# A fused convolution-attention and transformer block: the attention of six images in one run of slots, in place of pairs of images

## The reference

```
# channel attention (8 heads of 24 channels): Gram matrix over the tokens, softmax, projection, residual
q, k, v = split(w_qkv @ x + b_qkv);  attn = softmax(l2norm(q) @ l2norm(k).T * temperature)
x = x + (w_proj @ (attn @ v) + b_proj)
t = tokens(x)                                        # 1024 x 192
# causal self-attention: 6 heads of 32
h = layernorm(t);  q, k, v = h @ Wq, h @ Wk, h @ Wv
att = softmax(where(causal, q @ k.T / sqrt(192), -inf));  t = t + att @ v
# feed-forward with sign weights, two clips by a maximum over a group of 6 images
t = t + quant(gelu(quant(layernorm(t) @ Wb1 + b1)) @ Wb2 + b2)
```

## Time and profile before

| | before |
|---|---|
| time, median of 3 runs | 4978.42 us (4969.53 to 4983.48) |
| the profiled execution: its own time | 4979.79 us |
| its span | 4978.0 us |
| busy PE, DVE, ACT, POOL | 4124.8, 3470.0, 2934.6, 773.7 us |
| mean granted TensorE clock | 0.945 of full |

### The profile page before, as it was taken

One profiled execution on the slowest core, in us unless ns is written; L12 is line 12 of the kernel. 1 busy time (PEld: TensorE's weight loads), 2 busy tenths in 40 slices (PEclk: granted clock), 3 DMA queues, 4 the chain that ended last, 5 costly groups with the idle time before them and its releaser, 6 DMA issues.

```text
span 4978.0 us, 116213 instructions
## 1 busy us (share of the span) xinstructions
PE 4124.8 (83%) x38848; PEld 2997.8 (60%) x38848; DVE 3470.0 (70%) x6999; ACT 2934.6 (59%) x6271; POOL 773.7 (16%) x671
## 2 busy tenths in 40 slices
PE   4988887869898876989887779889876989897778
PEld 2766664556666545766664556666545766664555
DVE  3767677757676786767678767677776767778666
ACT  1555556846555575555566845555575555566745
POOL 0000002600000144000002600000143000002600
PEclk8999998989999998999998989999988999998989
DMA  2111111011121101111111011121101111111011
GB/s 59 40 34 33 34 39 26 0 46 33 34 57 35 33 0 39 33 34 33 40 33 26 0 46 33 37 56 33 33 0 39 33 34 34 39 33 26 0 39 39
DMA packets 46377, 161.59 MB, mean 32 GB/s; under 512 B 10098, under 2 KB 10612, under 8 KB 45684
## 3 DMA queue, kind: packets, MB, share of 16 engines
q1 hardware_dynamic: 45812, 154.38, 13.2%
HBM read 28.52 MB, written 25.17 MB: 11 GB/s over the span
## 4 chain that ended last, share of the span: by engine, by line
issue 78%; POOL 13%; PE 5%; DVE 2%; POOLq 1%; ACT 1%; DMA 0%; SPq 0%; DVEq 0%; ACTq 0%
POOL work L508 7%; POOL hi_z L478 2%; POOL hi_z L497 1%; POOL rstd L473 1%; POOL rstd L493 1%; PE S L691 1%; POOL NK L468 1%; PE PT L763 1%; PE PT L655 1%; PE OUT L675 1%; PE S L699 0%; DVE work L364 0%; DVE nmax L1114 0%; DMA B<-in_b 0%; PE S L641 0%
## 5 line engine op out<-in xcount | busy, mean ns | idle before, releaser
L870 ACT ACTIVATE work<-S,nmax 128x256 f32<-128x256 f32 (+7 forms) x1536 | 1138.8, 742 | 1114.6 <-DVE nmax L1114 1054.8
L1114 DVE TENSOR_REDUCE nmax<-S 128x1 f32<-128x256 f32 (+7 forms) x1536 | 1156.2, 753 | 851.0 <-PE S L643 835.2
L655 PE MATMUL PT<-ident,work 128*128 128x128 f32 x6912 | 1114.5, 282 | 214.8 <-DVE work L364 185.8
L655 PEld LDWEIGHTS PT<-ident,work 128*128 128x128 f32 x6912 | 749.7, 142 | 430.4 <-DVE work L364 260.9
L364 DVE COPY work<-PT 128x512 f32<-128x512 f32 (+3 forms) x1536 | 891.9, 581 | 57.7 <-PE PT L655 52.7
L691 PE MATMUL S<-odd,W1b 128*128 (+1 forms) x2160 | 529.0, 401 | 74.5 <-DVE work L1187 67.0
L508 POOL TENSOR_TENSOR work<-work 128x512 f16<-128x512 f32 x360 | 414.0, 1158 | 147.4 <-ACT work L916 133.0
L691 PEld LDWEIGHTS S<-odd,W1b 128*128 128x128 f16 x2160 | 214.4, 102 | 359.3 <-DVE work L1187 97.7
L641 PE MATMUL S<-KS,QS 128*128 128x512 f16 (+3 forms) x1152 | 334.5, 346 | 104.5 <-issue 56.0
L468 POOL TENSOR_TENSOR NK<-NK,halfneg 96x4 f32<-96x4 f32 x32 | 32.5, 1016 | 2188.0 <-DVE NK L1036 2188.0
L874 ACT ACTIVATE work<-PT 128x512 f32<-128x512 f32 (+3 forms) x768 | 331.3, 431 | 53.5 <-PE PT L655 53.4
(11 more groups left out here) (189 smaller groups left out, 6375.2 us busy)
## 6 DMA issues: line engine op xcount, KB each, us to landing
X<-in_x SPq DMA_DIRECT2D x32, 768.0 KB, 5.4
odd<-hi_z SPq DMA_DIRECT2D x128, 192.0 KB, 4.2
odd<-odd SPq DMA_DIRECT2D x128, 192.0 KB, 4.2
out_y<-work SPq DMA_DIRECT2D x64, 384.0 KB, 3.1
QS<-hi_z SPq DMA_DIRECT2D x64, 192.0 KB, 3.7
QS<-odd SPq DMA_DIRECT2D x64, 192.0 KB, 4.1
KS<-hi_z SPq DMA_DIRECT2D x64, 192.0 KB, 4.7
KS<-odd SPq DMA_DIRECT2D x64, 192.0 KB, 4.7
```

The source lines that it names most:

```text
L655: last = tr(bank[:, P * (j - c0):P * (j - c0) + P], PS[m % 2][:, m // 2 % 2, P * j:P * j + P], ident[:, :])
L870: A(PS[n % 2][:, n // 2 % 2, 0:w], S[:, n % 2, 0:w], ACT.Exp, bias=nmax[:, n % MAXES:n % MAXES + 1], accum_out=rowsum[:, sum_col(n):sum_co ...
L1114: v.tensor_reduce(nmax[:, n % MAXES:n % MAXES + 1], S[:, n % 2, 0:P * (qtile(n) + 1)], AX.X, ALU.max, negate=True).then_inc(max_made, 1)
```

## The change

- The loop body is a group of six images (216 slots for units, then 4 to drain); the last two images have a shorter one. An image has 36 slots.
- A slot holds one large unit or two small ones. Of six slots, four are large units (positions 0, 1, 3, 4), two are pairs of small ones (2, 5): each round of six slots takes the eight units `combos(11 - r)` and `combos(r)`. Each slot has two banks of `S`; the two halves of `S` alternate. One maximum instruction serves both units of a pair.
- TensorE transposes the tiles of slot n-2 at slot n. ScalarE copies the first four tiles of a large unit, ahead of its exponential of the slot; VectorE copies the others and those of the small pairs.
- PV takes four units at a time in four column groups: the four large ones of a round at slot 7 after its start, the four small ones at slot 8. Outputs leave in three batches of 128 x 512 an image, where there were four of 96 x 512.
- The front has the one bank `FR`. Each step waits for the release of the step before it. A step stands at the start of a slot (a whole number in the table: right behind the scores) or at its end (a half). VectorE's part of a `qk` step comes half a slot after TensorE's.
- The first scores of an image wait for both halves of the stacking (`stacked[0]` and `stacked[1]`).
- Tokens of images 1 to 5 of a group are written to T1 directly; QKL moves into XT; the spare part of `odd` holds the small pairs' exponentials.

The core of the diff:

```diff
-TILES = [(1, 7), (3, 5), (0, 6), (2, 4)]
-AHEAD = 3
-PV_AT = (8, 11)
-OT_AT, BACK_AT = 18, 19
+IMAGE = 36
+AHEAD = 2
+LARGES = (0, 1, 3, 4)
+SMALLS = (2, 5)
+PV_AT, OT_AT, BACK_AT = (7, 8), 15, 16
...
+def combos(grp):
+    return [divmod(4 * grp + i, NH) for i in range(4)]
+def slot_units(n):
+    r, p = n % IMAGE // 6, n % 6
+    if p in SMALLS:
+        i = 2 * SMALLS.index(p)
+        return [(r, i), (r, i + 1)]
+    return [(11 - r, LARGES.index(p))]
...
-SLOTS = {"xt0": 0, "xt1": 1, "xt2": 2, "xt3": 4, "g0a": 5, "g0": 6, "g1a": 7, "g1": 8, "wg0": 9, "wg1": 10,
-         "na": 11, "rb": 15, "u": 18, "mt": 19, "t0": 20, "t1": 21, "t2": 22, "t3": 23, "z0": 31, "z1": 32,
-         "z2": 33, "z3": 34, "qk0": 35, "qk1": 36, "qk2": 37, "qk3": 38, "qk4": 39, "qk5": 40, "v0": 41, "v1": 42,
-         "v2": 43, "v3": 44}
+SLOTS = {"xt0": 0, "xt1": 0.5, "xt2": 1.5, "xt3": 2, "g0a": 3, "g0": 3.5, "g1a": 4.5, "g1": 5, "wg0": 6, "wg1": 7,
+         "na": 8, "rb": 10.5, "u": 13.5, "mt": 14.5, "t0": 15.5, "t1": 16, "t2": 17, "t3": 17.5, "z0": 23, "z1": 23.5,
+         "z2": 24.5, "z3": 25, "qk0": 26, "qk1": 26.5, "qk2": 27.5, "qk3": 28, "qk4": 29, "qk5": 29.5, "v0": 30.5,
+         "v1": 31, "v2": 32, "v3": 32.5}
...
-        FB = [FR[:, :], S[:, 0, 512:1024]]
...
 (TensorE, front_part)
-                    if i >= 2:
-                        wait_freed(pe, pair, u, STEPS[i - 2])
+                    if i >= 1:
+                        wait_freed(pe, g, u, STEPS[i - 1])
...
 (TensorE, attention)
-                        if n % 24 == 0:
-                            pe.wait_ge(stacked[n % UNITS // 24], after(pair, u, STACKS, STACKS))
+                        if n % IMAGE == 0:
+                            for st in stacked:
+                                pe.wait_ge(st, after(g, u, STACKS, STACKS))
...
+                        for j in range(units[-1][0] + 1):
+                            for i, (qt, h) in enumerate(units):
+                                if j <= qt:
...
+                                    last = mm(OUT[32 * i:32 * i + 32, o:o + P], V[u % 2][:, j, D * h:D * h + D],
+                                              p_turned(m)[:, P * t:P * t + P], start=(j == 0), stop=(j == qt),
+                                              tile_position=(0, 32 * i))
```

More of the change, by code:

```diff
@@ new lines, in large_of, with pair_of, batch_groups, place @@
+def large_of(n):
+    return n // 6 * 4 + LARGES.index(n % 6)
+def pair_of(n):
+    return n // 6 * 2 + SMALLS.index(n % 6)
+def batch_groups(i):
+    return [2 * i, 2 * i + 1, 10 - 2 * i, 11 - 2 * i]
+def place(grp):
+    i = min(grp, 11 - grp) // 2
+    return batch_groups(i).index(grp)
+def sum_col(grp, i):
+    return 16 * (min(grp, 11 - grp) // 2) + 4 * place(grp) + i
+def chunks_of(n):
+    tiles = len(slot_units(n)) * (qtile(n) + 1)
+    per = 3 if tiles == 6 and not is_large(n) else 4
+    return [(t, min(per, tiles - t)) for t in range(0, tiles, per)]
@@ L106, in transposed, with last_slot, turned @@
+def last_slot(images):
+    return IMAGE * (images - 1) + 12 * (BATCHES - 1) + BACK_AT
+def turned(images):
     out = []
-    for slot in range(LAST_SLOT + 1):
+    for slot in range(last_slot(images) + 1):
         m = slot - AHEAD
-        if 0 <= m < U2:
-            out += [(slot, "p", m, c0, min(4, qtile(m) + 1 - c0)) for c0 in range(0, qtile(m) + 1, 4)]
-        out += [(slot, "o", j, 0, 0) for j in batches_at(slot, BACK_AT)]
-    return out
-CHUNKS = transposed()
-PT_PER = len(CHUNKS) // 2
@@ L117, with batches_at, groups_at @@
-assert len(CHUNKS) % 2 == 0
+        if 0 <= m < IMAGE * images:
+            out += [(slot, "p", m, t, k) for t, k in chunks_of(m)]
+        out += [(slot, "o", j, 0, 0) for j in batches_at(slot, BACK_AT, images)]
+    return out
+def batches_at(slot, at, images):
+    return [j for j in range(BATCHES * images) if 12 * j + at == slot]
+def groups_at(slot, images):
+    return [(2 * r + k, r % 6 if k else 11 - r % 6) for r in range(6 * images) for k in range(2)
+            if 6 * r + PV_AT[k] == slot]
@@ L120 @@
+GROUP = 6
+TURNED = {images: turned(images) for images in (2, GROUP)}
+PT_PER = len(TURNED[GROUP]) // 2
+assert len(TURNED[GROUP]) == 2 * PT_PER
 STEPS = ["xt0", "xt1", "xt2", "xt3", "g0", "g1", "wg0", "wg1", "na", "rb", "u", "mt", "t0", "t1", "t2", "t3",
@@ L346, in fronts_at, with after, wait_freed, of_group @@
-        def fronts_at(slot, run, parts, fronts):
+        LAST = NGROUPS
+        def after(g, u, per, n):
+            return g * (GS * per) + (u * per + n)
+        def wait_freed(e, g, u, step, less=0):
+            e.wait_ge(front_free, after(g, u, FRONT_FREES, freed(step) - less))
+        def of_group(g, per, n):
+            return g * (GS * per) + n
+        def of_turned(g, n):
+            return g * PT_PER + n
+        def fronts_at(slot, late, run, parts, fronts):
             for u in range(fronts):
@@ L369, in alone, with last_chunk, chunks_at @@
+        def last_chunk(m, images):
+            return max(i for i, c in enumerate(TURNED[images]) if c[1] == "p" and c[2] == m)
+        def chunks_at(n, images):
+            return [(i, c) for i, c in enumerate(TURNED[images]) if c[0] == n]
         def alone(e):
@@ L410, in _, with body @@
             front(0, 0, True)
-            def pair_body(pair, p):
-                for u in range(2):
-                    front(pair, u + 1, True)
+            def body(g):
+                for u in range(GS):
+                    front(g, u + 1, True)
             def group_tail(g):
@@ L481, in _, with body @@
             front(0, 0)
-            def pair_body(pair, p):
-                for u in range(2):
-                    front(pair, u + 1)
+            def body(g):
+                for u in range(GS):
+                    front(g, u + 1)
             def group_tail(g):
@@ L853, in _, with attention @@
                 front_part(name, 0, 0)
[L855 to L858 removed]
+            def attention(g, images, fronts):
+                for n in range(last_slot(images) + 1):
+                    for j in batches_at(n, OT_AT, images):
+                        act.wait_ge(pv_made, of_group(g, 12, 4 * (j + 1)))
```

425 lines of the change are left out of this document (200 added, 225 removed).

## The result

| | before | after |
|---|---|---|
| time, median | 4980.95 us (4 runs, 4969.53 to 4985.40) | 5205.21 us (4 runs, 5200.80 to 5207.40) |
| the profiled execution's span | 4978.0 us | 5202.3 us |
| mean granted TensorE clock | 0.945 | 0.912 |

The ratio is 1.0453, with a 95% interval of 1.0433 to 1.0472: slower by 224 us, where 5005 us were forecast.

What follows compares the result with a forecast made beforehand. TensorE, busy 83% of the span, was taken as the bound. Groups at 668.3 us against 666 gave +12, with the ends +23, on 4979.8: 5003, stated as 5005 us; range 4860 to 5130.

Steps and rivals of the forecast that it cites:

- the front ahead of everything: Work before the first image's scores: one bank puts steps in series, first scores wait for all transfers; +20 us.
- the last two images: The last pair: its first image goes from 107.5 to 110.5 us, the last gains some 12; −9 us.
- the price of the one bank and of the wait for all transfers: Costs at `qk`, image starts and the front: 10.6 us behind `qk0`, 2 of clock per start, 20 in the front.
- the waits pile up: Rival, slower: one-bank front steps hold back queues, first stretch stays 75 us, every start loses 3.4; 5175 us, chance 0.20.
- The ring's rival: Rival, faster: the large units' ring of scores, maximum, exponential explains most waits; first stretch 66 us, 4835 us, chance 0.32.
- The stretch from first scores to `qk0`: First part of an image: 70.6 us, 8.6 less than 79.2, with the clock's 2 us per start counted separately.
- The stretch from `qk0`: From `qk0` to the next image's first scores: 37.9 us, 10.6 more than 27.3; bounds 34 and 40.
- The walk of the queues: Slot by slot through the serial `qk` steps, slots 26 to 29: 22.4 us from `qk0` to the first transfer.
- PV: Attention's PV matmuls, units in fours: eight steps still 1.95 us, 4.1 us less on TensorE an image.
- The rival of the four column groups: Rival, slower: in PV four column groups are no better than three, a step 0.29 us; 5130 us, chance 0.08.
- The gap: TensorE idle 3 us ahead of each image's first scores, ended by a transfer, with a clock under 1 behind.
- The last image of a group: No wait for transfers: 70.6 + 35.2 to the end of its slots + 10 drain = 115.8 us.

Runs made afterwards that it cites:

- both_halves_before: The kernel before with an image's first scores waiting for all sixteen transfers, nothing else changed: 5095.47 us, ratio 1.022.
- fill: The change with 15 matmuls of 512 columns into the idle front bank ahead of each wait for the stacking inside a loop body: 5168.84 us, ratio 1.0377.
- one_bank_before: The kernel before with its front in the one bank FR, each step waiting for the release of the one ahead: 5382.73 us, ratio 1.081.
- two_stage: The change with stacking issued in two stages, two thirds after qk3's part and a third after qk5's, in 32 smaller transfers: 5143.51 us, ratio 1.0319.

## Why the prediction was wrong

The direction was right and the size was not: +23 us in the forecast's sum, +224 measured. In the forecast's own terms an image inside a group took 6.0 us more than forecast (25 times that is 149 us: 92 from the stretch behind `qk0`, 57 from the one ahead of it), a group's last image with its tail 9.7 (48 us together), the front ahead of everything 10.5 and the last two images 9; 15 us go off for the image before, which was taken as 110.0 us.

**The step that failed is the price of the one bank and of the wait for all transfers.** The forecast has 25 × 10.6 behind `qk0`, 26 × 2 of clock and 20 in the front, some 340 us. The two edits alone in the kernel before cost 399 and 112 us, 511 together, of which 9.6 and 3.3 us an image lie behind `qk0`. If they add, the gains were some 290 us, about 30 under the forecast's 315, and the costs 170 over it: most of the miss of 201.

The rival **the waits pile up** (5175 us, 0.20) came nearest in time, and only in part in form. It has 75 us and 3.4 of clock for the first stretch, which took 74.9 with the clock in it, and it leaves at 37.9 the second stretch, where most was lost. The ring's rival (66 us) is out.

- **The stretch from first scores to `qk0`** (70.6 us and 2 of clock; 74.9). Under-sized by 2.3 us, and made up wrongly: work too small, waits too large. I had TensorE's own work there at 58.8 us and waits at 11.5 (which add to 70.3, not 70.6). In the image of the windows above, the starts of successive matmuls that lie over 0.45 us apart are nine, 8.3 us together, so some 7 us of waits; all the other distances make 66.3 us, which with the clock's 1.5 taken off is some 65. Counted in the same way, the 25 images before have on average 18.5 long distances, 14.1 us together, and 65.3 us in short ones, those of the change 9.8, 9.5 us together, and 65.4 us in short ones. With those of its second stretch its waits were some 12 us in a pair's first image, not the 17 that I had made from 89 us of work, so less could be had by removing them. The waits that went are 3 to 4 us; that they are the ring's was argued, not shown. PV took less and the short distances did not shrink; some of them now lie at the half clock of round 3, and how much that is stays open. The clock at the start was 1.5 us of the 2.
- **The stretch from `qk0`** (37.9; 41.6 on average). The largest term of the miss. The walk of the queues was right to half a microsecond at the full clock, 22.9 us for 22.4, with the output batch between `qk2` and `qk3` as it said; the clock that falls there in 11 images, which was missing from it, makes the average 23.7. From the first transfer to the first scores the forecast had 15.5 us from the earlier trace rows, and 17.2 were measured on average; the first mask comes another 0.7 us later. both_halves_before was missed by as much, with a gap of 5.2 us for 3.6.
- **What the sum was.** I wrote that bank and transfers eat the 100 us of the drains. The forecast came near nothing as the difference of two terms of over 300 us each, so that a cost half as large again as I had it made nine times the loss. The 22.4 us for the walk, which were right, did not help: what a second bank had been worth could not be read from any row, and in the kernel before, with a slot for each step, TensorE waits as long without it (469.0 us) as in the change (471.8).
- **PV** (1.95 us for eight steps of four units). Right: the timeline of the change has

```profile
176.45 1.95 PE L725 MATMUL OUT<-work,V 128*32 128x128 f32 x64
```

  64 instructions where three units have 48, in the same time. All PV together keeps TensorE busy for 471.6 us where it was 603.2, 4.1 less an image, as forecast (busy and times of PV over the span, before and after):

```profile
0.00:4978.00 4978.00, 603.17 (x13824) 469.65 (x13824) 0.94 0.14 32
0.00:5202.40 5202.40, 471.59 (x13824) 370.51 (x13824) 0.91 0.13 31
```

  The rival of the four column groups is out.
- **The gap** (3 us, by the last transfer; 3.3). Right. Behind it the granted clock was 0.50 for a time in 24 of the 25 starts, and 1.00 in the tenth image's, shown above. The Trainium skill, "TensorE: Matmul & The Clock Gate", section "HAM oscillation — how this bites in real kernels", has a kernel with one such wait per tile fall back to the half rate every time; the trace agrees but for that one start. The 3.4 us that a start would have cost by the earlier trace rows were 1.5 (fill). Nor was the earlier trace rows's the one gap of this length in the kernel before: the restart of a pair in the earlier trace rows has 3.27 us, and behind it the clock was low for ten, so the drains that were spared held a price of the clock too:

```profile
344.00:354.00 10.00, 9.00 (x44) 6.46 (x44) 4.58 (x8) 6.01 (x15) 0.00 (x0) 0.52 0.01 3
```
- **The last image of a group** (115.8; with its tail 9.5 us over before, where 0.2 under it was forecast). The turned output that ends it came 120.1 us after the first mask, where before it came after 112.3; I had left out the clock and the slower first stretch there. The rest of the 9.5, 1.8 us, is the tail and the start behind it.
- **The front ahead of everything** (+20; +30.5). one_bank_before has 24.5 of it for 14 forecast, both_halves_before 6.7 for 6. The series of `xt`, `g`, `t`, `z` and `qk` was the under-sized term.
- **The last two images** (−9; 0). The last one gained 8.2 us where 12 were forecast (from its first mask to its last, 70.2 for 78.2); the one ahead of it takes 115.8 for 107.5, 8.3 more where 3 were forecast, and loses it again.

## What to carry to other kernels

A buffer's price is the time from its first write to its last release, with every queue in between, against the spacing of its users, and it can be read by taking the buffer away in the old kernel. When a wait is mended and little comes of it, look for the next one right behind it before giving the mend up: spreading the `qk` steps gave 9 us alone and 70 on top of the earlier stacking. Work of an engine counted from its instructions came out some 6 us an image too small here; the distances of starts in the trace, short and long ones apart, give work and waits in one count.

## What was not expected of the hardware

SyncE issued a transfer of 64 or 128 KB every 0.63 us in two_stage, so 32 of them took 20 us where 16 of 192 KB had taken 16.9 with their landing. TensorE's clock fell to 1.2 GHz (0.50 granted) at 24 of 25 gaps of 3.2 to 4.2 us and stayed at 2.4 GHz at one of 3.2. In 11 images it also fell in the `qk` stretch, where the longest distance between two matmuls was 2.3 us, as in this image of the change, and in 14 with the same distance it did not. TensorE had been busy 2.4 to 2.8 of 5 us for ten us ahead of the fall:

```profile
1550.00:1555.00 5.00, 2.37 (x12) 1.08 (x13) 2.66 (x5) 1.98 (x4) 0.00 (x0) 1.00 0.00 0
1555.00:1560.00 5.00, 2.80 (x19) 1.67 (x17) 3.14 (x6) 1.57 (x3) 0.00 (x0) 1.00 0.00 0
1560.00:1565.00 5.00, 3.47 (x13) 1.96 (x14) 2.49 (x4) 2.61 (x6) 0.00 (x0) 0.62 0.01 2
```
